# Second half of an attention and routed-FFN kernel: another order of bias sum, inverse roots and table steps, and integer token numbers

## The reference

```python
x = _layernorm(x + attn(x))                       # eps 1e-5, no scale
expert_idx = argmax(softmax(x @ Wr.T))
inter = sum_e (expert_idx == e) * gelu(x @ W1[e] + b1[e])     # 256 -> 1024
y = inter @ Wo + bo + x                           # 1024 -> 256
f = (y - mean(y)) * rsqrt(var(y) + 1e-12) * gamma + beta
out = _layernorm(x + f)                           # eps 1e-5
```

## Time and profile before

| | us |
|---|---|
| median of 3 runs | 532.12 |
| lowest, highest | 528.19, 534.21 |
| the profiled execution, own time | 528.38 |
| its span | 526.7 |
| busy: PE, DVE, ACT, POOL | 489.4, 431.5, 356.5, 315.4 |

### The profile page before, as it was taken

The page is one execution under the profiler, slowest core; times in us unless marked ns, Lnnn a source line. Parts: engine busy times, 40 slices in busy tenths (PEclk is TensorE's granted clock), DMA queues, the critical chain, the costliest instruction groups (busy, mean ns, idle before and its releaser), DMA issues. The chain is left out here.

```text
span 526.7 us, 24512 instructions
## 1 busy us (share of the span) xinstructions
PE 489.4 (93%) x8574; PEld 432.2 (82%) x8574; DVE 431.5 (82%) x1132; ACT 356.5 (68%) x796; POOL 315.4 (60%) x553
## 2 busy tenths in 40 slices
PE   6989999999999999899978898999999999999980
PEld 5878888788888888688866787888999989999970
DVE  6558798878987898669898567999999989999983
ACT  5677778777876878467867664566667757666860
POOL 8612446444464545434634347777888878888883
PEclk9999999999999999989999898999999999999996
DMA  8687688786977797768772122222235554442200
GB/s 200 165 245 198 185 220 205 204 217 180 259 211 213 196 255 197 188 191 222 174 205 72 44 61 62 71 64 63 77 105 183 206 182 162 163 147 71 53 25 7
DMA packets 90184, 80.96 MB, mean 154 GB/s; under 512 B 36502, under 2 KB 83871, under 8 KB 90018
## 3 DMA queue, kind: packets, MB, share of 16 engines
q1 hardware_dynamic: 86720, 70.95, 48.9%
q0 software_dynamic: 3248, 8.41, 4.7%
q10 hardware_dynamic: 98, 0.04, 0.0%
HBM read 43.50 MB, written 23.55 MB: 127 GB/s over the span
## 5 line engine op out<-in xcount | busy, mean ns | idle before, releaser
L1415 PE MATMUL ps<-v_even,w_hi 128*128 128x128 f16 x1024 | 142.1, 220 | 0.6 <-issue 0.3
L1397 PE MATMUL ps<-wo_hi,ks 128*128 128x256 f16 (+1 forms) x576 | 129.2, 274 | 6.4 <-DVE ks L1091 6.1
L834 ACT ACTIVATE probs<-ps,b1T 128x128 f32<-128x128 f32 (+1 forms) x312 | 85.8, 361 | 66.9 <-PE ps L1415 66.7
L1415 PE MATMUL ps<-v_even,w_lo 128*128 128x128 f16 x512 | 108.6, 220 | 0.1
L1415 PEld LDWEIGHTS ps<-v_even,w_hi 128*128 x1024 | 97.2, 98 | 3.4 <-issue 1.3
L1162 DVE TENSOR_REDUCE mx<-ps 128x4 bf16<-128x512 f32 x128 | 82.5, 682 | 3.7 <-PE ps L1466 2.5
L1397 PE MATMUL ps<-wo_lo,ks 128*128 128x256 f16 (+1 forms) x288 | 78.9, 274 | 0.0
L1091 DVE TENSOR_TENSOR ks<-probs,ks 128x512 f16<-128x512 f32 (+1 forms) x72 | 70.9, 985 | 5.9 <-ACT ks L841 5.6
L853 ACT ACTIVATE probs<-ps 128x512 f32<-128x512 f32 x128 | 69.5, 610 | 5.3 <-PE ps L1492 4.4
L1515 PE MATMUL ps<-v_odd,probs 128*64 128x17 f32 x1024 | 69.4, 210 | 2.0 <-issue 2.0
L744 POOL CAST att_hi<-att 128x256 f16<-128x256 f32 x27 | 10.7, 395 | 100.9 <-DVE att L1219 100.9
(11 more groups left out here) (248 smaller groups left out, 1283.3 us busy)
## 6 DMA issues: line engine op xcount, KB each, us to landing
qk_s<-qk_room SPq DMA_DIRECT2D x32, 256.0 KB, 2.7
w_in<-in_L_ffn_W_dram SPq DMA_DIRECT2D x16, 512.0 KB, 5.7
v_odd<-slots SPq DMA_DIRECT2D x64, 128.0 KB
qs<-qk_s SPq DMA_DIRECT2D x16, 384.0 KB
ks<-qk_s SPq DMA_DIRECT2D x16, 384.0 KB, 5.5
ks<-qk_s SPq DMA_DIRECT2D x32, 144.0 KB, 3.2
v_even<-v_odd SPq DMA_DIRECT2D x63, 68.0 KB, 3.1
qk_s<-qk_room SPq DMA_DIRECT2D x32, 128.0 KB, 2.7
```

What stands on the lines that cost most here:

```text
L834: last = nc.scalar.activation(g[1 - p][:, ic, n * w:(n + 1) * w], ps_h[1 - p][:, half, col + n * w:col + (n + 1) * w], ACT.Gelu, bias=b1T[ ...
L1397: ins = mm(ps_y[p][0:m], h[p][hs][:, ic, 0:m], wo[ws][:, ic, :], start=n == 0, stop=n == 3 * IC - 1)
L1415: up_ins = mm(ps_h[1 - p][:, half, col + m * w:col + (m + 1) * w], weights(ws, m, k, ic), sT[1 - p][ss][:, k, at], start=k + n == 0, stop= ...
```

## The change

The change touches the second half, and how token numbers are kept.

- GpSimd: the bias sum of slot j moves into `add_biases(j)` and gets a wait for the first split of slot j (`hl_done` at 2j + 1). The sums of slots 0 and 1 stand in the last steps of the first half. The two inverse roots of one turn, that of y2 of slot j-1 and that of z of slot j-2, are made by one sum and one power of two columns; the root of z is thus made a turn later than before, in the turn that uses it.
- VectorE: the order of a turn becomes y2, its statistics, low part of the input, second split, table step 0, ng, table step 1, fin, table step 2, z, table step 3, statistics of z, first split.
- Token numbers are integers in the same 4 bytes. The cast to integers goes, the scatter reads the loaded tile itself, and there are four buffers for it, each freed by the landing of the scatter of four slots earlier.
- The dispatch scatters of tiles 30 and 31 (`send_rows`) move on the POOL queue from before turn 2 to behind turn 2 and behind turn 3.

The diff, cut to its core:

```diff
-        token = [sb(f"token{k}", [P, 2], f32) for k in range(2)]
-        token_i = [sb(f"token_i{k}", [P, 1], i32) for k in range(2)]
+        token = [sb(f"token{k}", [P, 2], f32) for k in range(TOKENS)]
+        token_i = [token[k][:, 1:2].bitcast(i32) for k in range(TOKENS)]
...
-        mv_a = sb("mv_a", [P, 2], f32)
-        mv_b = sb("mv_b", [P, 2], f32)
-        ve_a = sb("ve_a", [P, 1], f32)
-        ve_b = sb("ve_b", [P, 1], f32)
-        rs_a = sb("rs_a", [P, 1], f32)
-        rs_b = sb("rs_b", [P, 1], f32)
+        mv = sb("mv", [P, 2, 2], f32)
+        mv_a, mv_b = (mv[:, n, :] for n in range(2))
+        ve = sb("ve", [P, 2], f32)
+        rs = sb("rs", [P, 2], f32)
+        rs_a, rs_b = (rs[:, n:n + 1] for n in range(2))
...
-                wait(sp, number_out, j - 1)
-                rows_of(token[p], j, C - 1, ROW, token_ld[p])
+                wait(sp, out_st[p], 16 * ((j - TOKENS) // 2 + 1))
+                rows_of(token[j % TOKENS], j, C - 1, ROW, token_ld[j % TOKENS])
...
+            def add_biases(j):
+
+                p, m = j % 2, rows_in(j)
+                pool.wait_ge(xr_ld[p], 16 * landed(j))
+                wait(pool, y2_done, j - 1)
+                wait(pool, z_done, j - 1)
+                pool.wait_ge(hl_done, 2 * j + 1)
+                nc.gpsimd.tensor_tensor(x_past[p][0:m], xr[p][0:m].unsqueeze(1).broadcast_to([m, 2, C]),
+                                        past_bias[0:m, :, :], ALU.add).then_inc(x_past_done, 1)
+
             def body3(j, p, load, up, down, norm, emit):
-                if down:
-                    pool.wait_ge(xr_ld[p], 16 * landed(j))
-                    wait(pool, y2_done, j - 1)
-                    wait(pool, z_done, j - 1)
-                    m = rows_in(j)
-                    nc.gpsimd.tensor_tensor(x_past[p][0:m], xr[p][0:m].unsqueeze(1).broadcast_to([m, 2, C]),
-                                            past_bias[0:m, :, :], ALU.add).then_inc(x_past_done, 1)
-                if norm:
-                    pool.wait_ge(mva_done, j)
-                    wait(pool, z_done, j - 1)
-                    m = rows_in(j - 1)
-                    nc.gpsimd.tensor_tensor(ve_a[0:m, :], mv_a[0:m, 1:2], eps_ffn[0:m, :], ALU.add)\
-                        .then_inc(vea_done, 1)
-                    pool.wait_ge(vea_done, j)
-                    nc.gpsimd.tensor_tensor(rs_a[0:m, :], ve_a[0:m, :], power[0:m, :], ALU.pow)\
-                        .then_inc(rsa_done, 1)
+                if down and j > 1:
+                    add_biases(j)
+                if norm or emit:
+
+                    kinds = slice(0 if norm else 1, 2 if emit else 1)
+                    m = rows_in(j - 2) if emit else rows_in(j - 1)
+                    if norm:
+                        pool.wait_ge(mva_done, j)
+                        wait(pool, z_done, j - 1)
+                    if emit:
+                        pool.wait_ge(mvb_done, j - 1)
+                        wait(pool, fin_done, j - 2)
+                    nc.gpsimd.tensor_tensor(ve[0:m, kinds], mv[0:m, kinds, 1], eps[0:m, kinds], ALU.add).then_inc(ve_done, 1)
+                    pool.wait_ge(ve_done, j)
+                    nc.gpsimd.tensor_tensor(rs[0:m, kinds], ve[0:m, kinds], power[0:m, kinds], ALU.pow).then_inc(rs_done, 1)
                 if emit:
                     apart(pool)
                     pool.wait_ge(fin_done, j - 1)
-                    pool.wait_ge(number_out, j - 1)
+                    pool.wait_ge(token_ld[(j - 2) % TOKENS], 16 * landed(j - 2, TOKENS))
                     m = rows_in(j - 2)
                     nc.gpsimd.indirect_dma_start(
-                        out=out_rows, out_offset=bass.IndirectOffsetOnAxis(ap=token_i[p][0:m, :], axis=0),
+                        out=out_rows, out_offset=bass.IndirectOffsetOnAxis(ap=token_i[(j - 2) % TOKENS][0:m, :], axis=0),
                         in_=fin[p][0:m], in_offset=None, bounds_check=N - 1, oob_is_err=False)\
                         .then_inc(out_st[p], 16)
-                if norm:
-                    pool.wait_ge(mvb_done, j)
-                    wait(pool, fin_done, j - 1)
-                    m = rows_in(j - 1)
-                    nc.gpsimd.tensor_tensor(ve_b[0:m, :], mv_b[0:m, 1:2], eps_outer[0:m, :], ALU.add)\
-                        .then_inc(veb_done, 1)
-                    pool.wait_ge(veb_done, j)
-                    nc.gpsimd.tensor_tensor(rs_b[0:m, :], ve_b[0:m, :], power[0:m, :], ALU.pow)\
-                        .then_inc(rsb_done, 1)
 
             for it in range(FIRST, LAST + 1):
                 if it == LAST - 1:
                     pool.wait_ge(ffn_w_ld, 16 * FFN_LOADS)
-                    slot_turn(body3, 0)
-                if it == LAST:
-                    slot_turn(body3, 1)
+                    add_biases(0)
...
+                if it == LAST - 1:
+                    add_biases(1)
                 n = it - 2
                 if a_tile(n):
                     pool.wait_ge(mv_done, n + 1)
...
+                if it == LAST - 1:
+                    slot_turn(body3, 1)
                 for n in (it - 3, it - 2) if it % 2 == 1 and a_tile(it - 2) and it - 3 >= ROWS else ():
...
-                    nc.gpsimd.tensor_tensor(row[n % ROWS][:, C:ROW], row[n % ROWS][:, C:ROW], ring_step[:, :], ALU.add)\
+                    nc.gpsimd.tensor_tensor(row_no[n % ROWS], row_no[n % ROWS], ring_step[:, :], ALU.add)\
                         .then_inc(number_done, 1)
-                if it % 2 == 0 and a_tile(it - 4):
+                if it % 2 == 0 and a_tile(it - 4) and it < LAST:
                     send_rows(it - 4)
-                if it == LAST:
-                    send_rows(it - 3)
                 if it == CONSTS_AT:
...
-            walk_slots(body3)
+            for j in range(2, SLOT_TILES + 2):
+                slot_turn(body3, j)
+                if j < 4:
+                    send_rows(TILES - 4 + j)
...
                     nc.vector.scalar_tensor_tensor(y2[0:m], ps_y[1 - p][0:m], W_DOWN, xbo[1 - p][0:m],
                                                    ALU.mult, ALU.add).then_inc(y2_done, 1)
-                    tables(j, 0)
                     dve.wait_ge(y2_done, j)
                     nc.vector.bn_stats(stats_a[0:m, :], y2[0:m]).then_inc(bna_done, 1)
-                    tables(j, 1)
                     apart(dve)
                     dve.wait_ge(bna_done, j)
-                    wait(dve, rsa_done, j - 1)
+                    wait(dve, rs_done, j - 1)
                     nc.vector.bn_aggr(mv_a[0:m, :], stats_a[0:m, :]).then_inc(mva_done, 1)
-                if down:
-                    split(j, p, 1)
-                if emit:
-                    dve.wait_ge(rsb_done, j - 1)
-                    wait(dve, out_st[p], 16 * ((j - 2) // 2))
-                    m = rows_in(j - 2)
-                    nc.vector.tensor_scalar(fin[p][0:m], z[0:m], mv_b[0:m, 0:1], rs_b[0:m, :],
-                                            ALU.subtract, ALU.mult).then_inc(fin_done, 1)
-                if norm:
-                    tables(j, 2)
                 if load:
                     dve.wait_ge(sh_done, j + 3)
                     wait(dve, h_done, 2 * j + 2)
                     m = rows_in(j + 2)
                     nc.vector.tensor_tensor(sT[p][1][:, :, 0:m], ps_sx(j + 2)[:, :, 0:m], sT[p][0][:, :, 0:m], ALU.subtract)\
                         .then_inc(sl_done, 1)
+                if down:
+                    split(j, p, 1)
                 if norm:
-                    apart(dve)
                     m = rows_in(j - 1)
-                    dve.wait_ge(token_ld[1 - p], 16 * landed(j - 1))
-                    wait(dve, out_st[1 - p], 16 * ((j - 1) // 2))
-                    nc.vector.tensor_copy(token_i[1 - p][0:m, :], token[1 - p][0:m, 1:2]).then_inc(number_out, 1)
+                    tables(j, 0)
                     dve.wait_ge(mva_done, j)
                     wait(dve, z_done, j - 1)
                     nc.vector.scalar_tensor_tensor(ng[0:m], y2[0:m], mv_a[0:m, 0:1], gam[0:m, :],
                                                    ALU.subtract, ALU.mult).then_inc(ng_done, 1)
-                    tables(j, 3)
-                    dve.wait_ge(rsa_done, j)
+                    tables(j, 1)
+                if emit:
+                    dve.wait_ge(rs_done, j)
+                    wait(dve, out_st[p], 16 * ((j - 2) // 2))
+                    m = rows_in(j - 2)
+                    nc.vector.tensor_scalar(fin[p][0:m], z[0:m], mv_b[0:m, 0:1], rs_b[0:m, :],
+                                            ALU.subtract, ALU.mult).then_inc(fin_done, 1)
+                if norm:
+                    m = rows_in(j - 1)
+                    tables(j, 2)
+                    dve.wait_ge(rs_done, j)
                     dve.wait_ge(ng_done, j)
                     wait(dve, fin_done, j - 1)
                     nc.vector.scalar_tensor_tensor(z[0:m], ng[0:m], rs_a[0:m, :], xbe[1 - p][0:m],
```

(2 more changed lines are left out.)

35 lines of the change are left out of this document (19 added, 16 removed).

## The result

The changed kernel took 525.0 us (median of 4 runs, 522.5 to 526.5) against 532.1 for the kernel before: a ratio of 0.9864, 95% interval 0.9815 to 0.9912. On a second occasion it was 0.9873 (0.9827 to 0.9919). It is faster by 1.3%. The profiled execution took 523.99 us, its span 522.3.

What follows compares the result with a forecast made beforehand. TensorE was taken to bound the plain turns, with VectorE late at hand-over and table turns. Gains 4.4 + 3.0 + 1.4 less 0.6 made 8.2 us, 1.55%, applied to the 532.12 median: 524 us, range 518.5 to 531.

Steps and rivals of the forecast that it cites:

- What bounds the kernel: Turns 10 to 30: TensorE sets the pace at 5.52 us a turn, so no gain expected in plain turns.
- Rival D: Plain turns: TensorE follows VectorE's and GpSimd's loop, so 0.2 us more in 25 turns, 519 us; chance 0.06.
- Blocking: VectorE and GpSimd keep each other off SBUF: 0.81 us of a plain turn, about 0.95 of a table step.
- Sum behind the first split, root pair: Each turn: second split unblocked, second root column 0.2 us, root wait 0.45; VectorE's loop 5.3 us, under TensorE's 5.52.
- Rival A: Only part of the gain, 3 to 6 us (526 to 529), from dear roots, longer output waits, table turns at 5.9; chance 0.2.
- Table steps: Turns 3 to 9: steps behind the second split no longer meet the sum; 6.08 to 5.65 us a turn, 3.0 gained.
- Hand-over: Turns 0 to 2: earlier sum and later scatters remove TensorE's waits and the clock drop; 4.4 us gained.
- Rival E: Hand-over gets no faster, VectorE being late by the last attention tile: 2 us less gain, 526; chance 0.08.
- Tokens: Turns 10 to 30: integer numbers and a ring of four remove the cast and VectorE's load wait; 1.4 us gained.
- End: Last turns: output step waits for the root, scatter stands ahead of the last root, dearer root; 0.6 us lost.
- Rival B: Output scatter holds the first split: 539 us, or 533 with the cheap root; chance 0.06 each.
- Rival C: One-input steps wait too: first statistics held until the sum's end, loop 5.9 us, 538; chance 0.02.

Runs made afterwards that it cites:

- sum_free: The changed kernel without the bias sum's wait for the first split, from slot 2 on; ratio 1.0585 to the kernel before.
- tables_old: The changed kernel with the table steps back in their old places in VectorE's turn; ratio 0.9915 to the kernel before.
- before_sum_waits: The kernel before, with only the bias sums of tiles 2 to 35 made to wait for the first split; ratio 1.0043 to the kernel before.
- scatters_turns67: The changed kernel with the two late dispatch scatters behind turns 6 and 7 in place of 2 and 3; ratio 0.9857 to the kernel before.
- scatters_inside34: The changed kernel with the two late dispatch scatters between root pair and output scatter of turns 3 and 4; ratio 0.9819 to the kernel before.
- handover_old: The changed kernel with GpSimd's old hand-over order (turn 1's sum and roots early, both late scatters ahead of turn 2); ratio 0.9939 to the kernel before.
- end_roots_first: The changed kernel with tile 34's outer root and tile 35's two roots alone, ahead of tile 34's scatter; ratio 0.9821 to the kernel before.
- scatters_inside: The changed kernel with the two late dispatch scatters between root pair and output scatter of turns 2 and 3; ratio 0.9858 to the kernel before.

## Why the prediction was right

The time (525.0 against 524) and the sign were right; in the profiled pair the gain from slot 0 on was 5.5 us, not 8.2, and the medians' gain of 7.1 stands between. The profile of before was one of that kernel's quick executions, 3.7 us under its median, and the attention half of the changed profile came 1.1 us late: 5.5 - 1.1 = 4.4 us is the difference of the two spans. I applied a ratio of 1.55% to the median where the steps support some 1.0% and the measured ratio is 1.36% with an interval that holds both ends. The time came out closer than the sum deserved.

*What bounds the kernel*: right. With 0.57 us of standing on VectorE and GpSimd's busy time down by a quarter, the plain turns stayed at 5.52. Rival D is out.

*Blocking*: right, and sharper than I had it. In four meetings the held instruction ends 0.55, 0.56 (turn 4 of the changed kernel) and 0.56 us (sum_free) after the sum, or 0.04 for a step of 8 columns (tables_old), whether its row starts before the sum's or after. By these rows VectorE is not slowed; it is stopped until the sum is over, and then takes its usual time.

*Sum behind the first split, root pair*: right in its effect, wrong in what brings it. I gave the new place to the wait. before_sum_waits shows the wait alone to do nothing, and its rows put the sum's late start down to the root that the pairing takes away; sum_free shows the wait then to be worth the whole change and 34 us more (254.7 us from slot 0 on, against 220.8 before and 215.3). The root's second column cost 0.12 to 0.15 us (0.72 against 0.60 and 0.57), where I took 0.2. The estimate of 0.45 us for waiting on the roots was too dear: of the 21 plain turns it is zero in 11, 0.22 us in eight and 0.62 in two. Rival A's causes are out, but its size isn't: it said a gain of 3 to 6 us, and the steps gave 5.5, by the scatters and the end.

*Table steps*: the term that was mis-sized, 3.0 forecast, 1.97 measured. Five of the seven turns averaged 5.57, under my 5.65. The step that failed is the sentence on the two late scatters, "that is inside the 5.65": they cost 0.59 and 1.08 us over 5.52, 1.67 together, which scatters_turns67 moved (turns 7 and 8 got 1.06 of it) and scatters_inside34 took away (1.63). No table step took over 0.23 us. Their place is worth more than I had summed: 3.05 us against tables_old.

*Hand-over*: 4.33 against 4.4, and full clock behind it, as forecast. The 0.3 for slot 0's first split lies ahead of its first output product, where these steps don't see it (TensorE stood 0.43 us there before and doesn't now), so like for like it is 4.33 against 4.1. handover_old confirms the place and shows that the other parts would have made it worse. Rival E is out.

*Tokens*: 0.67 in this pair, 0.86 alone, 1.4 forecast. The arrival wait is gone, but I had filled the stage's excess over 21 x 5.52 with it. 0.2 of that excess is the two table transposes, and three further turns took 5.70 to 5.75 us with no wait shown, TensorE's products standing 0.06 us further apart behind the turn's start. Why they do is open.

*End*: -1.48 against -0.6, outside the bounds. The direction and both mechanisms were right; I gave the wait for the pair 0.25 and it is 0.89, for it stands behind slot 35's statistics, and I gave the scatter ahead of the last root 0.15 where it costs some 0.5 (that root's sum begins 0.58 us behind its statistics, 0.09 before), and I didn't see that the residual of slot 35 comes 0.25 us later too (4.38 us after the slot's first output product, 4.13 before). end_roots_first gets 0.95 of it back.

*Rival B* (the scatter meets the split): didn't come in the changed kernel. The split of turn 29 starts 0.42 us after the scatter and takes 0.69. Its "point of decision" between 0.37 and 0.46 us into a scatter was a misreading: what decides is what stands behind the scatter. From 296 us on, the fourteen profiles have 500 VectorE steps with both inputs in SBUF that started while GpSimd's scatter ran. With no bias sum directly behind the scatter, all 451 took their usual time, at 0.37 us and at any other. With one, 38 of 49 were held until the sum was over. Of the 11 that weren't, ten were splits that the sum itself waited for, and one had started 0.12 us into the scatter. sum_free made such a meeting of almost every turn. *Rival C* is out: all 33 full-width first statistics from turn 3 on took 0.43 us, 31 of them with the sum beside them. The Trainium skill's GPSIMD Engine Reference, Key points, names two kinds of VectorE instructions that contend; the changed kernel's trace agrees for two SBUF inputs (the splits of turns 3 and 4) and has no held instruction of one.

## What to carry to other kernels

Find which instructions of one engine stop another (they can do it before their own row begins, when nothing but the instruction ahead keeps them), and give them places by order first and by a wait second: measure the wait in the order that it will stand in, since alone it may show nothing and in the new order it may hold the kernel together. When steps are paired to save instructions, look at the last turns, where the pair makes the older half wait for the newer. When work moves out of a busy place, count what stands right behind it in its new place, turn by turn; an average over turns hides it.

## What the runs showed of the hardware

A VectorE split of 0.69 us took 2.48 when it started 0.64 us before a bias sum of 1.28 us that stood directly behind a scatter (sum_free): it was over 0.56 us after the sum, so the whole instruction was late, not its rest. Of the 38 steps that were held this way, six would by their usual length have been over 0.04 to 0.44 us before the sum's row begins. Whether the sum's hold starts before its row does, or the scatter's last part is what holds, no row says; a scatter with no sum directly behind it held none of 451.

In scatters_inside ScalarE stood 2.38 us with "remote" as its releaser, and in scatters_turns67 1.03 us (before 349.74). Each stop began 0.5 to 0.6 us after a dispatch scatter had, at 321.67 and 348.20; from slot 0 on, no other profile of the study has such a row, though all have dispatch scatters. The queues of scatters_inside between 323.5 and 324.5 us (queue, packets, MB, share of the 16 DMA engines):

```profile
q0 software_dynamic: 25, 0.04, 10.8%
q14 instruction: 1, 0.01, 5.7%
```

The Trainium skill's Runtime: NRT & Kernel Launch, Instruction fetch mechanics, says that an engine's sequencer fetches its next page over a DMA queue of its own while it executes, "mostly hidden". A late fetch would be a candidate for the stop, but the rows don't bear it out. The block of instructions above starts after 324.3 us and takes 0.91 us (5.7% of 16 engines' 1 us), so it is still under way when ScalarE goes on at 324.65; in scatters_turns67 the nearest block starts after 347.6 and takes 0.45 us, so it is over before the stop begins at 348.71. What ScalarE stood for is open.
